# Two graph-attention and expert layers on one core: the scores are read from PSUM, routing steps are dropped, spare products are put around TensorE's waits, and ScalarE weights one of two results

## The reference

```python
x = x + gnn(layernorm(x), adj)     # h = x W; e = leaky_relu(src_i + dst_j, 0.2); masked softmax; h' = alpha h
x = x + ffn(layernorm(x))          # top 2 of 8 experts: gelu(xe W1 + b1) W2 + b2, weighted and added
```

## Time and profile before

| What | Value |
|---|---|
| Median of 3 runs | 965.69 us (958.6 to 968.75) |
| Time of the profiled execution | 966.77 us |
| Its span | 964.9 us |
| Busy: PE, PEld, DVE | 688.7, 562.8, 734.9 us |
| Busy: ACT, POOL | 499.7, 556.4 us |

### The profile page before, as it was taken

One profiled execution on the slowest core, in us unless ns is written; L12 is line 12 of the kernel. 1 busy time (PEld: TensorE's weight loads), 2 busy tenths in 40 slices (PEclk: granted clock), 3 DMA queues, 4 the chain that ended last, 5 costly groups with the idle time before them and its releaser, 6 DMA issues.

```text
span 964.9 us, 23945 instructions
## 1 busy us (share of the span) xinstructions
PE 688.7 (71%) x6353; PEld 562.8 (58%) x6384; DVE 734.9 (76%) x2554; ACT 499.7 (52%) x1129; POOL 556.4 (58%) x544
## 2 busy tenths in 40 slices
PE   3877788550999999999977878987305777777600
PEld 2655466450999999998455656776204655566400
DVE  6678988752899999998478888887544788788628
ACT  2556655410777777775146655556304655555334
POOL 0036777775376677767100766666772777777720
PEclk9978977855999999999987777668657999999855
DMA  8373333332233323326432444222232333333757
GB/s 220 110 168 111 104 96 97 91 98 73 67 94 86 87 81 85 88 78 174 142 103 82 132 141 140 86 83 67 69 116 73 103 107 96 96 100 102 234 224 315
DMA packets 129397, 111.45 MB, mean 116 GB/s; under 512 B 30306, under 2 KB 112681, under 8 KB 129352
## 3 DMA queue, kind: packets, MB, share of 16 engines
q1 hardware_dynamic: 112072, 77.04, 28.6%
q0 software_dynamic: 17280, 33.87, 10.7%
HBM read 60.32 MB, written 52.36 MB: 117 GB/s over the span
## 4 chain that ended last, share of the span: by engine, by line
PE 32%; DVE 25%; issue 19%; POOL 12%; ACT 6%; DMA 4%; SPq 1%; POOLq 1%; DVEq 1%; ACTq 0%
PE bank L628 9%; PE bank L642 9%; POOL row_buf L456 6%; POOL y_buf L464 5%; PE bank L519 5%; DVE stat L906 3%; PE bank L516 3%; ACT xn L703 2%; PE bank L500 2%; DMA y_buf<-g_y,g_dst 2%; DVE xin L977 2%; DVE yin L969 2%; DVE x1w L996 2%; PE bank L614 2%; DVE e_msk L956 1%
## 5 line engine op out<-in xcount | busy, mean ns | idle before, releaser
L456 POOL DMA_INDIRECT row_buf<-pay,slot x256 | 264.0, 1031 | 233.4 <-DVE slot L1070 155.2
L464 POOL DMA_INDIRECT y_buf<-g_y,g_dst x284 | 292.2, 1029 | 135.9 <-issue 86.1
L808 ACT ACTIVATE g_xT<-bank 128x512 f16<-128x512 f16 x142 | 84.9, 598 | 167.4 <-PE bank L614 165.2
L628 PE MATMUL bank<-g_xT,w 128*128 128x256 f16 x1278 | 169.0, 279 | 1.7 <-ACT g_xT L808 1.0
L628 PEld LDWEIGHTS bank<-g_xT,w 128*128 x1278 | 118.8, 100 | 20.9 <-issue 2.8
L614 PE MATMUL bank<-ident,g_in 128*128 128x128 f16 x568 | 57.4, 225 | 84.6 <-DMA g_in<-row_buf 73.4
L815 ACT ACTIVATE xn<-bank,b_cols 128x256 f32<-128x256 f32 x216 | 86.8, 474 | 23.9 <-PE bank L628 16.0
L642 PE MATMUL bank<-w,g_h 128*128 x1260 | 85.7, 221 | 18.9 <-DVE g_y L1218 18.7
L642 PEld LDWEIGHTS bank<-w,g_h 128*128 128x128 f16 x1260 | 76.8, 98 | 28.4 <-issue 26.3
L815 ACT ACTIVATE xt<-bank,b_cols 128x256 f32<-128x256 f32 x210 | 84.4, 475 | 15.7 <-PE bank L628 12.1
L614 PEld LDWEIGHTS bank<-ident,g_in 128*128 128x128 f16 x568 | 37.2, 100 | 92.9 <-issue 72.1
(11 more groups left out here) (194 smaller groups left out, 1365.2 us busy)
## 6 DMA issues: line engine op xcount, KB each, us to landing
g_in<-row_buf SPq DMA_DIRECT2D x142, 130.0 KB, 2.2
yin<-y_buf SPq DMA_DIRECT2D x20, 512.0 KB, 5.3
x_buf<-x1w SPq DMA_DIRECT2D x16, 520.0 KB, 5.2
xin<-x_buf SPq DMA_DIRECT2D x10, 520.0 KB, 4.3
y_buf<-g_y,g_dst POOLq DMA_INDIRECT x284
xin<-in_x_dram SPq DMA_DIRECT2D x8, 512.0 KB
adj_in<-in_adj_dram SPq DMA_DIRECT2D x16, 256.0 KB, 3.6
row_buf<-pay,slot POOLq DMA_INDIRECT x256, 2.6
```

The costliest lines, as they stand in the source:

```text
L456: pool.indirect_dma_start(row_buf[L][:, :], bass.IndirectOffsetOnAxis(ap=slot[q][:, k, t:t + 1], axis=0), pay[q][:, t, :], None).then_inc( ...
L464: pool.indirect_dma_start(y_buf[L][:, :], bass.IndirectOffsetOnAxis(ap=g_dst[k][:, t:t + 1], axis=0), g_y[k][:, t, :], None, bounds_check= ...
L628: last = nc.tensor.matmul(dst, w[:, bass.ds(e * (2 * HID[L]) + (wp * HID[L] + c * P), P)], g_xT[q][:, xp, :], start=(m == 0), stop=(m == 2))
L808: nc.scalar.activation(g_xT[q][:, :, :], x_ps[q], ACT.Copy).then_inc(s.gT_sb, 1)
```

## The change

- **Scores.** ACT no longer copies the scores to `e_sb`. DVE waits for PE itself and reads bank 2 in the first of the same four instructions. Masking now comes first, with the mask value divided by 0.2, and the leaky part second.
- **Order on DVE.** `arrive` of n+2 stands ahead of `scores` of n+1, except in the first step.
- **Weights in layer 1.** DVE's `arrive` multiplies only the second result (128x1024); ACT multiplies the first (`scale_first`, 8 instructions, at the head of its step for block n+1). `take_in` adds the second result first and then waits for `y0_scaled`.
- **Routing.** `tok_run` is gone: the token numbers stay in `pay` and are raised by 2048 there at each use. The maximum itself is written as the expert's mark, and `place` compares with `grp_m` (8 minus the expert) for it. The two products for `hot_pos` are one. For layer 1 the numbers are written anew by `file_under`, which stands after layer 0's blocks and ahead of `group_tables`; since it writes to `pay`, it waits for all scatters of layer 0.
- **Unread products.** In layer 1, PE waits for `st1` of block n+1 (DVE's first statistics) and then runs 8 of them (`IDLE_ST1`). At the head of both group stages it runs 96 of them, after `tables`, `w_ready`, the load of two expert numbers, and POOL's beginning of the last block.
- **Groups.** SP reads the row numbers of the first four groups before it waits for the scatters. DVE finishes group 0 before it places and splits group 2.

```diff
@@ groups (sync)
+                early = [sp.value_load(grp_ri[0:1, k:k + 1], min_val=0, max_val=ROWS - GRP) for k in range(AHEAD)]
                 for q in range(2):
                     sp.wait_ge(s.scattered[q], 16 * TOP * TILES * NBLK // 2)
...
@@ step (tensor)
                     keep_busy(IDLE_ATT[L])
+                    if L == 1 and not last:
+                        pe.wait_ge(SL[L].st1, n + 2)
+                        keep_busy(IDLE_ST1)
...
@@ groups (tensor)
                 pe.wait_ge(s.tables, 1)
                 pe.wait_ge(w_ready[L], 1)
+                es = experts(0, 2)
+                pe.wait_ge(pool_turns, L * (NBLK + NG) + NBLK)
+                with pe.Fori(0, IDLE_GROUPS // IDLE_LOOP):
+                    keep_busy(IDLE_LOOP)
                 for k in range(2):
                     to_feature_rows(k, 0)
-                es = experts(0, 2)
...
@@ blocks (scalar)
+            def scale_first(L, n, q, turn):
+                act.wait_ge(SL[L].x_in[q], 64 * (turn + 1))
+                for t in range(TILES):
+                    last = nc.scalar.activation(yin[q][:, 0, t, :], yin[q][:, 0, t, :], ACT.Copy, scale=xin[q][:, t, 0:1])
+                last.then_inc(SL[L].y0_scaled, 1)
...
                 def step(i, d, first=False, last=False):
                     n, q, turn = block_at(i, d)
+                    if L == 1 and not (first or last):
+                        scale_first(L, *block_at(i, d + 1))
                     attention(L, n, first)
...
-                    if not last:
-                        copy_scores(L, n + 1)
...
@@ file_under (vector)
+            def file_under(numbers):
+                for q in range(2):
+                    last = V.tensor_scalar(pay[q][:, :, D], numbers, float((q - 2) * BLK), None, ALU.add)
+                return last
...
@@ scores (vector)
-                dve.wait_ge(s.e_copied, n + 1)
-                ch.did(V.scalar_tensor_tensor(e_act[:, :], e_sb[:, :], 0.2, e_sb[:, :], ALU.mult, ALU.max))
-                ch.wait()
-                ch.did(V.scalar_tensor_tensor(e_msk[:, :], keep[:, :], MASKED[L], e_act[:, :], ALU.add, ALU.min))
+                dve.wait_ge(s.e_ps, n + 1)
+                ch.did(V.scalar_tensor_tensor(e_msk[:, :], keep[:, :], MASKED[L] / SLOPE, bank[2][:, :], ALU.add, ALU.min))
+                ch.wait()
+                ch.did(V.scalar_tensor_tensor(e_act[:, :], e_msk[:, :], SLOPE, e_msk[:, :], ALU.mult, ALU.max))
...
@@ take_in (vector)
-                    for k in range(TOP):
+                    for k in (1, 0):
                         ch.wait()
+                        if k == 0:
+                            dve.wait_ge(s.y0_scaled, n + 1)
...
@@ route, places (vector)
-                V.tensor_copy(pay[q][:, :, D], tok_run[:, :])
+                V.tensor_scalar(pay[q][:, :, D], pay[q][:, :, D], 2.0 * BLK, None, ALU.add)
...
-                        V.tensor_scalar(tok_run[:, :], tok_run[:, :], float(BLK), None, ALU.add)
-                        V.tensor_scalar(pay[q][:, :, D + 1], r1[:, :], -1.0, float(NE), ALU.mult, ALU.add)
...
-                for k in range(TOP):
-                    V.tensor_tensor(hot_pos[:, k, :, :], hot[:, k, :, :], pos[:, :, :], ALU.mult)
+                V.tensor_tensor(hot_pos[:, :, :, :], hot[:, :, :, :], pos[:, :, :].unsqueeze(1).to_broadcast([P, TOP, TILES, NE]), ALU.mult)
...
@@ end of the vector program, between blocks(L) and group_tables(L)
                 if L == 0:
                     V.memset(h_sb[:, :, H_END:H_END + 1], 1.0)
-                    ch.did(V.tensor_copy(tok_run[:, :], cst[:, C_TOK:C_TOK + TILES]))
+                    for q in range(2):
+                        dve.wait_ge(SL[0].scattered[q], 16 * TOP * TILES * NBLK // 2)
+                    ch.did(file_under(cst[:, C_TOK:C_TOK + TILES]))
                 group_tables(L)
                 split_first(L)
```

More of the change, by code:

```diff
@@ L46 @@
 BIG = 3.0e38
+SLOPE = 0.2
 RT_BITS = 1598872064.0
@@ L49 @@
 IDLE_EXP, IDLE_ATT = [10, 0], [7, 8]
-IDLE_START, IDLE_LOOP = 112, 8
+IDLE_START, IDLE_LOOP, IDLE_ST1, IDLE_GROUPS = 112, 8, 8, 96
 C_ID, C_TRI, C_REV, C_TOK, C_BASE, C_G, C_END = 0, 128, 256, 320, 328, 336, 336 + NG
@@ L96, in __init__ @@
         self.att_ps, self.att_sb = sem(f"att_ps{L}"), sem(f"att_sb{L}")
-        self.rinv_ready = sem(f"rinv_ready{L}")
+        self.rinv_ready, self.y0_scaled = sem(f"rinv_ready{L}"), sem(f"y0_scaled{L}")
         self.xt_ready, self.xtT_ps, self.xtT_sb = sem(f"xt_ready{L}"), sem(f"xtT_ps{L}"), sem(f"xtT_sb{L}")
@@ L181, in gnn_moe_kernel @@
         keep = sb("keep", [P, TILES * NODES])
-        e_sb = sb("e_sb", [P, TILES * NODES])
         e_act = sb("e_act", [P, TILES * NODES])
@@ L197, in gnn_moe_kernel @@
         slot = [sb(f"slot{q}", [P, TOP, TILES], U32) for q in range(2)]
-        tok_run = sb("tok_run", [P, TILES])
-        tok_lane = sb("tok_lane", [P, 1])
+        tok_lane = sb("tok_lane", [P, 1 + TILES])
         base_run = [sb(f"base_run{L}", [P, NE]) for L in range(2)]
         lg, eq1, ca, lg2, eq2, cb = (sb(n, [P, TILES, NE]) for n in ("lg", "eq1", "ca", "lg2", "eq2", "cb"))
-        l_max, r1, l_max2, r2 = (sb(n, [P, TILES]) for n in ("l_max", "r1", "l_max2", "r2"))
+        l_max, l_max2, r2 = (sb(n, [P, TILES]) for n in ("l_max", "l_max2", "r2"))
         hot = sb("hot", [P, TOP, TILES, NE])
@@ L227, in gnn_moe_kernel @@
         past_n = sb("past_n", [P, NG, NE])
-        grp_e, grp_b, grp_c, grp_r = (sb(n, [P, NG]) for n in ("grp_e", "grp_b", "grp_c", "grp_r"))
+        grp_e, grp_m, grp_b, grp_c, grp_r = (sb(n, [P, NG]) for n in ("grp_e", "grp_m", "grp_b", "grp_c", "grp_r"))
         grp_ei, grp_ri = sb("grp_ei", [P, NG], I32), sb("grp_ri", [P, NG], I32)
@@ L392, in groups @@
                 for k in range(AHEAD):
-                    load_group(k, k)
+                    load_group(k, k, early[k])
                 def load_next(g, k):
@@ L788, in blocks @@
                 load_table(ACT.Exp)
+                if L == 1:
+                    scale_first(L, *block_at(0, 0))
                 norm_input(L, 0, 0)
+                if L == 1:
+                    scale_first(L, *block_at(0, 1))
                 input_columns(L, 0)
-                copy_scores(L, 0)
                 step(0, 0, first=True)
@@ L869, in _ @@
             V.tensor_copy(tri16[:, :], cst[:, C_TRI:C_TRI + P])
-            ch.did(V.tensor_scalar(tok_lane[:, :], cst[:, C_TOK:C_TOK + 1], TILES - 1.0 / P, None, ALU.mult))
+            ch.did(V.tensor_scalar(tok_lane[:, 0:1], cst[:, C_TOK:C_TOK + 1], TILES - 1.0 / P, None, ALU.mult))
             ch.wait()
-            V.tensor_scalar(tok_run[:, :], cst[:, C_TOK:C_TOK + TILES], 1.0 / P, tok_lane[:, 0:1], ALU.mult, ALU.add)
+            ch.did(V.tensor_scalar(tok_lane[:, 1:], cst[:, C_TOK:C_TOK + TILES], 1.0 / P, tok_lane[:, 0:1], ALU.mult, ALU.add))
+            ch.wait()
+            file_under(tok_lane[:, 1:])
             for L in range(2):
@@ L967, in arrive @@
                 if L == 1:
-                    weights = xin[q][:, :, 0:TOP].rearrange("p t k -> p k t").unsqueeze(3).to_broadcast([P, TOP, TILES, D])
-                    ch.did(V.tensor_tensor(yin[q][:, :, :, :], yin[q][:, :, :, :], weights, ALU.mult))
+                    weights = xin[q][:, :, 1:2].to_broadcast([P, TILES, D])
+                    ch.did(V.tensor_tensor(yin[q][:, 1, :, :], yin[q][:, 1, :, :], weights, ALU.mult))
             def take_in(L, n, q, turn):
@@ L1023, in route @@
                 yield
-                for k, (val, vmax, eq, cand, cmax) in enumerate(((lg, l_max, eq1, ca, r1), (lg2, l_max2, eq2, cb, r2))):
-                    ch.did(V.tensor_reduce(vmax[:, :], val[:, :, :], AX_X, ALU.max))
+                for k, (val, vmax, eq, cand, cmax) in enumerate(((lg, l_max[:, :], eq1, ca, pay[q][:, :, D + 1]), (lg2, l_max2[:, :], eq2, cb, r2[:, :]))):
+                    ch.did(V.tensor_reduce(vmax, val[:, :, :], AX_X, ALU.max))
                     yield
-                    ch.did(V.tensor_tensor(eq[:, :, :], val[:, :, :], bc(vmax[:, :]), ALU.is_equal))
+                    ch.did(V.tensor_tensor(eq[:, :, :], val[:, :, :], bc(vmax), ALU.is_equal))
                     yield
@@ L1096, in step @@
                     finish_steps(placing)
-                    if not (last or over):
+                    if first:
                         scores(L, n + 1)
@@ L1100, in step @@
                         arrive(L, *block_at(i, d + 2))
+                    if not (first or last or over):
+                        scores(L, n + 1)
                 arrive(L, 0, 0, 0)
@@ L1231, in turn @@
                         g, a = SPAN * i + k, (k + 2) % AHEAD
+                        very_first = isinstance(g, int) and g == 0
+                        if very_first:
+                            finish(0, 0, 0, es[0])
                         if not last or k + 2 < n:
@@ L1234, in turn @@
                             split(g + 2, a)
-                        finish(g, k % AHEAD, per_turn * i + k // AHEAD, es[k])
```

(2 more changed lines are left out.)

20 lines of the change are left out of this document (9 added, 11 removed).

## The result

The changed kernel takes 983.47 us (median of 4 runs, 981.28 to 987.51), the kernel before 965.63 in the same rounds (958.6 to 968.75). The ratio is 1.0208, with a 95% interval of 1.0151 to 1.0265: slower, by about 2%. The profiled execution spans 981.0 us against 964.9, 16.1 more.

A forecast was written before the change was run, and what follows sets the result against it. It took POOL to bound layer 0's blocks and layer 1's groups, PE layer 0's groups, and a ring through all engines layer 1's blocks. +28.0 - 9.3 - 1.5 = +17.2 us gave 983 us, range 971 to 996.

The forecast's parts named there:

- The wait ahead of the tables: Between layer 0's blocks and groups: tables, paddings and split wait for the last landing; layer 0 costs +28.0 us.
- Landing: End of layer 0's blocks: the last index scatter lands at 231.3 us instead of 235.8.
- The waits: Layer 0's blocks: POOL's waits for blocks 1 and 5 shrink by 2.4 and 2.1 us, after which it is never idle.
- the clock gave back: Layer 0's groups: they now begin at 2.4 GHz, which returns 2.8 us (bounds 1 and 3).
- Layer 1's blocks: Ring through all engines: 1.1 us less a block, -9.3 us for the stage (bounds -1 and -11).
- the start of the stage: Start of layer 1's blocks: block 1's scores come when DVE is free, 3.5 us gained in all.
- the wait for ACT's weighting: Layer 1's blocks: DVE, after adding the second result, waits 1.5 us for `y0_scaled`.
- that rival: Layer 1's clock is not held: blocks cost 0.2 us each instead of gaining, 992 us; chance 0.14.
- The rival that VectorE alone bounds the blocks: Layer 1's blocks: ACT is not late, the ring is 22.3 us, 972 us in all; chance 0.10.
- No surcharge for PSUM: Layer 1's scores: DVE's one instruction reading PSUM costs nothing extra; the skill's table would give an estimated 0.065 us.
- Layer 1's groups: First groups of layer 1: POOL's first scatter of results starts at 740.5 against 741.93, -1.5 us (bounds -3.5 and +17).
- The last stage: End of the kernel, behind layer 1's groups: it keeps its length.

The follow-up runs named there:

- the 8 products alone: Kernel before, plus only 8 unread PE products ahead of the scores of layer 1's blocks and the wait placing them: 954.0 us, ratio 0.9922.
- VectorE weights both: Changed kernel, but VectorE multiplies both results by their weights again, and ACT neither weights the first nor is waited for: 976.31 us, ratio 1.0124.
- the wait alone: Kernel before, plus only a VectorE wait for layer 0's index scatters ahead of the group tables: 979.17 us, ratio 1.0145.

## Why the prediction was right

**The wait ahead of the tables: right, the one step that decided.** Landing: 231.3 forecast, 229.93 measured (227.65 + 2.28). The first scatter came 1.4 earlier, for 1.5. The waits gave 2.2, for 3.0: POOL did wait again, for blocks 2 and 4, where the forecast had it never idle. That scatters took 17 ns less each in the mean, 2.1 us for 128, was not forecast; without it the landing would have come 0.7 later than forecast, and not 1.4 earlier. That the landing was forecast so closely is in part luck. From the landing to `w_ready` 14.1 us for 14.4, to the first product 1.6 for 1.3, the products 22.6 for 22.7, and the clock gave back 2.9 for 2.8. The errors add up to the 1.45 by which layer 0 came out cheaper: +26.55 for +28.0. Both directions of the test agree: putting the wait behind the split in the changed kernel gave 27.6 us, adding it to the kernel before, which has no products behind it, moved the groups by 15.6.

**Layer 1's blocks: the sum right, its parts not told apart.** Five blocks gained 6.8 for 5.5, and the start of the stage 3.8 for 3.5. The forecast took the gain to be 1.1 a block, made of a shorter way for the scores and half a weighting on ACT, with the clock as a condition. The runs split it otherwise, over five periods:

| step | runs | five periods, us | each |
|---|---|---|---|
| clock held at the scores | before, then the 8 products alone | 129.35 to 118.15 | -2.2 |
| the rest of the change: scores from PSUM, order on DVE, routing steps | these, then VectorE weights both | 118.15 to 116.2 | -0.4 |
| first result weighted by ACT | this, then the changed kernel | 116.2 to 122.57 | +1.3 |

So the clock brought more than the whole gain. What the parts of the middle row are worth singly, no run tells. The chain itself was forecast well: from the end of the second statistics to the last addition 8.77 us forecast (567.5 - 558.73), 8.74 measured (555.72 to 564.46). In it the wait for ACT's weighting was seen and sized too small (1.5 for 2.5), because DVE got through its scores and the first addition sooner than forecast. Its meaning was missed: with the clock held, the kernel before has no such wait and is faster by 0.9 us a block than the changed one.

Here the right sum is in part luck. The forecast starts from rows in which the scores ran at 0.50. Had the profiled execution of before run as the one with the wait alone did (117.69 us for five periods), the changed kernel's blocks would have come out 4.9 us slower, where the forecast has 5.5 faster.

**The bounds of that rival.** With the clock not held, the forecast had 0.2 a block above the period of before, so 26.0. The run without the 8 products had 26.0 to 26.6 in three of five blocks. The rival that VectorE alone bounds the blocks did not hold in the changed kernel; it comes close to holding as soon as VectorE weights both (22.0 us of work in 23.1), at 23.1 and not 22.3.

**No surcharge for PSUM.** `e_msk`, now with one source in PSUM, takes 0.68 us, and the next instruction starts 0.71 behind its start. In the kernel before, the same operation with both sources in SBUF (L956, at 561.69) takes 0.69, and the next one starts 0.73 behind it. The forecast had taken no surcharge. The 0.065 us that it estimated from the Trainium skill ("VectorE: DVE Perf Modes", the section on the TRN2 errata) are not there.

**Layer 1's groups.** The time from `g_k` to the first real product was 23.9 us (725.58 to 749.51) for 24.0. The first scatter followed 7.1 later, where 5.4 + 0.4 + 0.9 had been taken. The last stage kept its length, as forecast: 39.9 us from the start of the last scatter of results to the end, before and after. The stage that did not is POOL's, from layer 1's first scatter of results to its last: 184.53 for 183.03, where the forecast had taken it as fixed. No run gives the cause; with the group code of before and no unread products there, it was 182.58 in the run with the wait alone and 185.72 in the one with the 8 products, so 1.5 us need none of the change.

## What to carry to other kernels

A wait costs what is queued behind it, so put it as late in its engine's order as the data allows; here the same wait cost 27.6 us with tables, split and unread products behind it, and nothing behind the split. Before an operation moves from the busiest engine to an idler one, follow what stands behind its new place: 1.1 us less on VectorE cost 1.3 a block. Unread products pay only up to the landing of what the next real product needs, and before a gain is put down to an edit, the clock in that stretch has to be the same in both traces.

## What was not expected of the hardware

- The granted clock of the same code can settle at either level: layer 1 of the kernel before had 0.50 at the scores of blocks 1 to 6 in one execution, and 1.00 at those of blocks 2 to 7 in the one with a wait added in layer 0; without the 8 products the changed kernel had both in one execution, with periods of both kinds.
- Indirect scatters of one shape took 992 ns in the mean before and 975 after, with single ones of 1.1 to 1.7 us (up to 1.56 after) among those of 0.96.
